# A graph network with a feed-forward part on chosen tokens: the choice made in two parts, the first during layer three

## The chip, the cores and the metric
The kernel runs on one core of a Trainium2 chip. The metric is the device time of one execution in microseconds (us). TensorE (PE) multiplies, VectorE (DVE), ScalarE (ACT) and GpSimd (POOL) do the rest of the arithmetic, SyncE (SP) issues most DMAs, GpSimd issues the indirect ones.

## What is computed
x has 6250 rows of 256. It is normalised, goes through three graph convolutions (200000 edges and a loop at each node), and is added to x. Then the rows are normalised again, half of them (less one) are chosen by a score, and these go through a feed-forward part and are added at their place:
```
x = x + gnn(layernorm(x))                    # relu after layers one and two
n = layernorm(x)
weights = n @ wr + br                        # one score a row
sel_idx = top_k(weights, 3125)[:3124]
h = gelu(n[sel_idx] @ w1 + b1)               # 256 -> 1024
y = (h @ w2 + b2) * weights[sel_idx]         # 1024 -> 256
out = x + n + zeros.at[sel_idx].set(y)
```

## The kernel before
The nodes are 49 tiles of 128 rows. A layer's sum over the edges is a product with the adjacency matrix: for the 32 or 34 fullest rows of tiles ("dense", 49 matmuls of 128x128 by 128x512 in f16 each) it is held as f16 tiles, for the others ("sparse") rows are gathered from DRAM by GpSimd (`fetch_row`, L1434) and summed with one-hot matrices (L958; the one-hots by VectorE at L753). One such matmul is a **unit**; a table puts 5798 units of the three layers in one order, dense and sparse ones mixed, and layer three begins at unit 3830. All that stands beside them is placed by unit numbers: the sum of a finished tile (`sum_tile`, L736 and L738) and the addition of x (`add_x`, L777 and L781) at `SUM_AT`, the loads for it (`fetch_extra`) at the sum of two tiles before. `norm_group` (L783 to L809, with a root on ScalarE, L1218) normalises a group of tiles right behind the sum of its last tile; the groups have `NORMS` = 7, 7, 7, 7, 7, 7, 5, 2 tiles in the order in which they end, and the sums that close them stand at units 4184, 4465, 4723, 5026, 5267, 5565, 5743 and 5798. 75 units later SyncE stores them (`store_pairs`, L1571 and L1572: normalised row and base row, side by side, into `pair_dram`). `sum_tile` frees the PSUM bank of its tile. All sparse tiles use one bank, so the start of a sparse tile waits for the sum of the sparse tile before it: the starts at units 5054, 5273, 5383, 5488, 5593 and 5699 wait for the sums at 5041, 5252, 5361, 5467, 5580 and 5677.

When the layer ends, the block of `graph` ends (every engine waits for all), and `finish` begins. SyncE loads w1 and w2 and stores out's base rows, 6.1 MB in one DMA (L1666, and L1668 for the rest). VectorE finds the score from which 3124 rows are chosen: it counts the scores above a bound (L1691), then in eight rounds above 15 (at last 7) trial bounds at once (L1696 to L1699); TensorE adds up the partitions (L1799), VectorE reads the counts (L1701 to L1703). Two matmuls (L1801, L1802) count ties and places, VectorE spreads each chosen row over slot numbers (L1709 to L1726, one-hot tiles at L1726), 49 matmuls (L1807) turn that into the list, and GpSimd gathers the listed rows of `pair_dram` (L1785), 25 slots of 128 rows (the last 52). The slots are taken in blocks of 1 and then 4 (`BLOCKS`). Per block: TensorE turns the rows (`turn`, L1816), VectorE copies them out of PSUM (`settle`, L1736), TensorE makes eight hidden sums (`hidden`, L1827, four PSUM banks), ScalarE gelu (L1864). Then the output sums of the block before (`outputs`, L1838, eight matmuls a slot), VectorE's gate (`weigh`, L1742 and L1744) and addition (`put`, L1749 and L1751), and GpSimd's store into out (L1791).

Of the kernel before, what the change touches and what calls it, by code (L numbers as in the profile page):

```python
# [8 lines left out]
ALU = mybir.AluOpType  # L9
ACT = mybir.ActivationFunctionType  # L10
AX = mybir.AxisListType
# [5 lines left out]
P = 128  # L17
# [116 lines left out]
NORMS = (7, 7, 7, 7, 7, 7, 5, 2)  # L134
# [4 lines left out]
BLOCKS = [range(0, 1)] + [range(c, min(c + BLOCK, SLOTS)) for c in range(1, SLOTS, BLOCK)]  # L139
BLOCK_OF = {s: (c, s - b[0]) for c, b in enumerate(BLOCKS) for s in b}  # L140
# [45 lines left out]
SUM_AT = sum_units()  # L186
TURN_AT = [u + 12 for u in SUM_AT]
# [82 lines left out]
PAIR_OUT_AT = [SUM_AT[2 * TILES + NORM_FROM[g + 1] - 1] + 75 for g in range(len(NORMS))]  # L270
# [17 lines left out]
BANK, BANK_BEFORE = bank_table()  # L288

# [17 lines left out]
def build(nc, x, x_turned, dst_rows, dst_over, dst_last, edges, gw, gb, wr, br, w1, b1, w2, b2, out):  # L307
    ctx = ExitStack()
    with ctx:
# [14 lines left out]
        with ExitStack() as inner:  # L324
            graph(nc, inner, space, gathered_in, ones, route, small, smalli, b1_sb, br_b, x, x_turned, dst_rows, dst_over, dst_last, edges, gw, gb, wr, br, b1, b2,
                  pair_dram)
        finish(nc, space, gathered_in, ones, route, small, smalli, pair_dram, br_b, w1, b1_sb, w2, out)


def graph(nc, ctx, space, gathered_in, ones, route, small, smalli, b1_sb, br_b, x, x_turned, dst_rows, dst_over, dst_last, edges, gw, gb, wr, br, b1, b2, pair_dram):  # L330
# [58 lines left out]
    def items_of(l):  # L389
# [17 lines left out]
    SLOT_OF = (3,) + tuple((TD - 4 + m) % ASLOTS for m in range(1, 4))  # L407
# [51 lines left out]

    (c_init, c_pool, c_dve, last_in, over_in, first_in, weights_in, later_in) = (sem(n) for n in (  # L460
# [25 lines left out]
    (m_v, m_p, stat_s, root_s, norm_s, pairs_out, x_added) = (sem(n) for n in (  # L486
        "m_max", "m_all", "stat_step", "root", "xn_ready", "pairs_stored", "x_added"))
# [19 lines left out]
    first_bank = [both[:, 0:D], ag[2][:, 0:D]]  # L507
    steps = {"all": 0}

    def bank(q):  # L510
        return (ag[0][:], ag[1][:], ag[2][:], pw[0][:, 0, :], pw[0][:, 1, :], pw[1][:, 0, :])[BANK[q]]

    with nc.Block() as block:
        @block.vector
        def _(dve):
# [12 lines left out]
            noted(dve.memset(ones16[:], 1.0), "ones")  # L528
            done(dve.memset(wrap[:], 0.0))
# [216 lines left out]
            def spot_steps(n):  # L746
                if n == 0:
                    dve.wait_ge(stored_0, 16)
                    dve.wait_ge(stored_s, 32)
                if n >= HOTS // 4:  # L750
                    dve.wait_ge(g_used, SPOT_GROUPS[n - HOTS // 4][1])
# [31 lines left out]
            def norm_group(g):  # L783
# [15 lines left out]
                if g:  # L799
# [1099 lines left out]
```

## Time and profile before
| | us |
|---|---|
| median of 3 runs | 2122.54 (2122.16 to 2124.14) |
| span of the profiled execution | 2111.3 |
| TensorE's matmuls busy | 1871.8 (89%) |
| VectorE busy | 1025.7 (49%) |
| ScalarE busy | 529.4 (25%) |
| GpSimd busy | 1152.2 (55%) |
| mean DMA rate | 190 GB/s |

The span is that of one execution, and the median is of other, unprofiled ones; 11.2 us lie between them. A profile is read from the page (shares of the whole span) to the views of single stretches: the chain of work that ended last names what released what; the windows give each engine's busy time in a stretch, with the clock that TensorE was granted (1.00 is 2.4 GHz, 0.50 is 1.2 GHz); the waits list what TensorE stood still for; the timeline lists instructions with their start, length, and in brackets the idle time before them and what ended it.

### The profile page before, as it was taken

The page shows a single profiled execution, that of the slowest core. Times are in us where ns is not written, and L with a number is a line of the kernel's source. Part 1 is how long each engine was busy: PE and PEld are TensorE (multiplying, and loading weights), DVE is VectorE, ACT ScalarE, POOL GpSimd, SP SyncE. Part 2 cuts the span into 40 slices and gives each one's busy share as a digit, 9 for nine tenths or more (in the row PEclk, how much of TensorE's full clock was granted, in tenths as well). Part 3 has the DMA queues.
Part 4 walks back from the last instruction along what each step waited for, and adds up shares of the span by engine and source line. Part 5 has one row for each costly group of instructions (what it writes and reads, how often), then busy time and mean ns, then how long its engine had stood idle before and what let it go on. Part 6 is the DMA issues. An engine that isn't in the chain of part 4 may idle for free. (4 is left out here: it accounts for less than half of the span.)

```text
span 2111.3 us, 28622 instructions
## 1 busy us (share of the span) xinstructions
PE 1871.8 (89%) x10097; PEld 1069.4 (51%) x10097; DVE 1025.7 (49%) x3169; ACT 529.4 (25%) x1126; POOL 1152.2 (55%) x1218
## 2 busy tenths in 40 slices
PE   6874879989999999897999999998999899828998
PEld 5752556655555566444554544443444344314666
DVE  7777888867666666322222222202555443572212
ACT  5814234433444455301111111100000000002110
POOL 5400656766676666134777777724777677404111
PEclk9965899999999999999999999999999999968999
DMA  7647045445555665745677677655888688454000
GB/s 253 201 149 267 16 152 172 155 156 165 166 198 195 197 204 179 268 161 177 227 237 243 223 231 244 228 170 195 290 287 291 209 293 289 151 196 124 21 15 24
DMA packets 166993, 402.10 MB, mean 190 GB/s; under 512 B 28651, under 2 KB 118945, under 8 KB 154056
## 3 DMA queue, kind: packets, MB, share of 16 engines
q1 hardware_dynamic: 116264, 262.16, 35.2%
q0 software_dynamic: 50592, 138.13, 21.3%
q8 instruction: 84, 1.38, 0.3%
q14 instruction: 53, 0.43, 0.1%
HBM read 284.18 MB, written 116.01 MB: 190 GB/s over the span
## 5 line engine op out<-in xcount | busy, mean ns | idle before, releaser
L1434 POOL DMA_INDIRECT space_rows<-row_dram,src_s x947 | 962.7, 1017 | 394.5 <-issue 209.9
L946 PE MATMUL ag<-space_a,space_ring 128*128 128x512 f16 x2107 | 628.7, 382 | 22.1 <-POOL space_ring L1442 22.1
L914 PE MATMUL pw<-space_tables 128*128 128x147 f16 (+1 forms) x2022 | 330.1, 248 | 53.7 <-DVE space_tables L714 45.2
L958 PE MATMUL ag<-space_rows,hots 128*128 128x512 f16 x947 | 359.7, 380 | 3.0 <-DVE hots L753 1.5
L914 PEld LDWEIGHTS pw<-space_tables 128*128 128x128 f16 x2022 | 219.1, 116 | 240.3 <-DVE space_tables L714 70.6
L714 DVE TENSOR_TENSOR space_tables<-iota_two,space_tables 128x294 f16<-128x294 f16 (+1 forms) x1011 | 304.7, 335 | 0.0
L1190 ACT ACTIVATE space_ring<-pw 128x784 f16<-128x784 f32 (+1 forms) x257 | 220.4, 858 | 309.4 <-PE pw L914 305.5
L946 PEld LDWEIGHTS ag<-space_a,space_ring 128*128 128x128 f16 x2107 | 198.8, 97 | 125.3 <-issue 19.4
L711 DVE TENSOR_TENSOR space_tables<-iota_many,space_tables 128x512 f16<-128x512 f16 x506 | 215.1, 425 | 52.0 <-PE pw L914 49.5
L946 PE MATMUL pw<-space_b,space_ring 128*128 128x512 f16 x784 | 205.2, 382 | 8.1 <-DVE space_work L738 8.1
L946 PE MATMUL pw<-space_a,space_ring 128*128 128x512 f16 x686 | 173.3, 385 | 0.0
L1200 ACT ACTIVATE space_work<-space_work,per_node 128x256 f32<-128x256 f32 x147 | 73.3, 503 | 315.0 <-DMA space_work<-extra 315.0
L958 PEld LDWEIGHTS ag<-space_rows,hots 128*128 128x128 f16 x947 | 107.3, 113 | 86.5 <-DMA space_rows<-row_dram,src_s 5.7
L743 DVE SCALAR_TENSOR_TENSOR space_a<-both,per_node,space_a 128x256 f16<-128x256 f32 x49 | 23.7, 484 | 230.4 <-ACT space_a L1214 230.4
L1208 ACT ACTIVATE space_work<-both,gb_sb 128x128 f32<-128x128 f32 x196 | 61.4, 364 | 250.8 <-PE both L964 250.7
L946 PEld LDWEIGHTS pw<-space_b,space_ring 128*128 128x128 f16 x784 | 77.2, 99 | 92.5 <-DVE space_work L738 8.6
L946 PEld LDWEIGHTS pw<-space_a,space_ring 128*128 128x128 f16 x686 | 67.9, 99 | 82.0 <-issue 5.3
L753 DVE TENSOR_TENSOR hots<-iota_many,key_s 128x512 f16<-128x512 f16 x238 | 105.9, 461 | 1.5
L946 PE MATMUL ag<-space_b,space_ring 128*128 128x512 f16 x392 | 105.0, 384 | 0.0
L1442 POOL TENSOR_TENSOR space_ring<-space_ring,ident 128x128 f16<-128x128 f16 x34 | 22.1, 652 | 150.6 <-ACT space_ring L1194 93.6
L972 PE MATMUL both<-gw_sb,space_work 128*128 128x256 f32 x392 | 101.4, 381 | 0.0
L1791 POOL DMA_INDIRECT out<-space_a,space_rows x24 | 23.4, 973 | 141.3 <-DVE space_a L1751 141.3
(351 smaller groups left out, 1895.4 us busy)
## 6 DMA issues: line engine op xcount, KB each, us to landing
space_ring<-adj SPq DMA_DIRECT2D x49, 1568.0 KB, 7.6
adj<-space_ring SPq DMA_DIRECT2D x34, 1568.0 KB, 6.1
space_tables<-adj SPq DMA_DIRECT2D x17, 1568.0 KB, 7.6
extra<-hots SPq DMA_DIRECT2D x3, 6272.0 KB, 23.1
space_work<-extra SPq DMA_DIRECT2D x147, 128.0 KB
space_rows<-row_dram,src_s POOLq DMA_INDIRECT x947, 3.8
space_b<-in_x_turned SPq DMA_DIRECT2D x7, 896.0 KB, 13.8
space_a<-in_x SPq DMA_DIRECT2D x7, 896.0 KB, 6.1
```

The costliest lines, as they stand in the source:

```text
L711: dve.tensor_tensor(olo[:, r // 2], iota_many[:], slo[:, 2 * j:2 * j + 4].unsqueeze(1).broadcast_to([P, P, 4]), ALU.is_equal)
L714: dve.tensor_tensor(ohi[:, r, 0:n], iota_two[:, 0:n], key[:, 2 * j:2 * j + 2].unsqueeze(1).broadcast_to([P, n, 2]), ALU.is_equal).then_inc ...
L743: dve.scalar_tensor_tensor(hh[l][:, t, D:2 * D], ph[:, 0:D], factor[:, l, t:t + 1], hh[l][:, t, 0:D], ALU.mult, ALU.subtract).then_inc(lo_ ...
L753: dve.tensor_tensor(hots_area[:, n % (HOTS // 4)], iota_many[:], key_s[:, s:s + 4].unsqueeze(1).broadcast_to([P, P, 4]), ALU.is_equal).the ...
L914: pe.matmul(pw[v % 2][:, half, at_c:at_c + n], olo[:, j % RING // 2, :, j % 2 * 2 + i], ohi[:, j % RING, 0:n, i], start=s == FIRST[w], sto ...
L946: mm = pe.matmul(bank(q), a[:, k, :], hh[l][:, k, :], start=i == 0 and not own, stop=i == TILES - 1)
L958: pe.matmul(bank(q), hots_area[:, hot_at, :, g - SPOT_GROUPS[SPOT_GROUP_OF[g]][0]], slots[g % GR], start=False, stop=i == n).then_inc(g_us ...
L972: mm = pe.matmul(ph[:, 0:D], fresh[:, q % 2, f, :], gw_sb[:, l, f, :], start=f == 0, stop=f == HALVES - 1)
L1190: act.activation(target[:, :, d:d + n].rearrange("p s (h d) -> p s h d", h=2), pw[v % 2][:, :, 0:n // 2 * TILES].rearrange("p h (d s) -> p ...
L1200: act.activation(ep[:, q % 2], ep[:, q % 2], ACT.Copy, scale=unfactor[:, l, t:t + 1]).then_inc(e_scaled, 1)
L1208: ins = act.activation(fresh[:, q % 2, f, :], px[:, f * P:(f + 1) * P], ACT.Relu, bias=gb_sb[:, l, f:f + 1])
L1434: pool.indirect_dma_start(slots[g % GR], None, row_dram[STEP_LAYER[g]], bass.IndirectOffsetOnAxis(src_s[:, s:s + 1], 0)).then_inc(g_in[g % ...
```

## The change
The first 38 tiles to be normalised (six groups) hold 38 tiles' scores; the 11 others have 1460 rows (tiles 27 to 33 and 45 to 48). Of the 38 tiles' rows the best 3124 - 1460 = 1664 (13 slots) belong to the chosen ones whatever the others' scores are. They are chosen during layer three (`begin_choice`, `after_count`, `spread` and `take_list` on VectorE, `count_choice`, `ties` and `listing` on TensorE, all with 0 for the first choice), at fixed units: counts at 5440, 5462 and so on to 5616, ties at 5638, the list at 5693, four turns at 5770 to 5788, their copies at 5792. The remaining 1460 rows (12 slots) are chosen from all the rest in the same manner, with the steps put between hidden sums and output sums of the first slots. The blocks are now 4, 3, 3, 3 slots and, of the second choice, 4, 4, 4. Turns of later slots stand behind single hidden sums or output sums (`TURN_IN_HIDDEN`, `TURN_IN_OUT`), hidden sums use three banks. `NORMS` is 7, 7, 7, 7, 5, 5, 7, 4, and the groups stand at 4184, 4465, 4723, 5026, 5204, 5382, 5696 and 5798; each is stored 70 units later, with a third DMA for each tile that stores out's base rows. There is one block for all: no barrier behind layer three. w1 and w2 are loaded at units 5686 and 5745. The late tiles' part of `pair_dram` is filled with zeros early on, so that every row holds a number.

The tables and the code of the engines, cut to its core:
```diff
-NORMS = (7, 7, 7, 7, 7, 7, 5, 2)
+NORMS = (7, 7, 7, 7, 5, 5, 7, 4)
+EARLY_GROUPS = 6
+EARLY = sum(NORMS[:EARLY_GROUPS])
...
+FIRST_SLOTS = (KEEP - UNSEEN) // P
+CHOSEN = (FIRST_SLOTS * P, KEEP - FIRST_SLOTS * P)
...
+COUNT_SPACE = 22
+COUNT_AT = [SUM_AT[2 * TILES + EARLY - 1] + 58 + COUNT_SPACE * r for r in range(COUNTS_OF_CHOICE)]
+TIES_AT = COUNT_AT[-1] + COUNT_SPACE
+LISTING_AT = TIES_AT + 55
+ROWS_TURN_AT = [UNITS - 28 + 6 * s for s in range(len(BLOCKS[0]))]
+ROWS_SETTLE_AT = UNITS - 6
...
-PAIR_OUT_AT = [SUM_AT[2 * TILES + NORM_FROM[g + 1] - 1] + 75 for g in range(len(NORMS))]
+PAIR_OUT_AT = [u + 70 for u in NORM_AT]
...
+            def after_count(ph, r):
...
+                dve.wait_ge(s_count, COUNTS_OF_CHOICE * ph + r + 1)
...
+                    dve.tensor_reduce(part[:, 0:n], flags[:, 0:n], AX.X, ALU.add).then_inc(s_part, 1)
...
+            def settle(s):
+                (c, i), n = BLOCK_OF[s], width(s)
+                if s == FIRST_SLOTS:
+                    dve.wait_ge(pairs_late, 48 * (TILES - EARLY))
+                dve.wait_ge(x_t, s + 1)
...
             upto(UNITS + 300)
+            begin_choice(1)
+            for c in range(len(BLOCKS) + 1):
+                if c < len(BLOCKS) and c != SECOND:
+                    hidden_turns(c)
+                for s in BLOCKS[c - 1] if c else ():
+                    weigh(s)
+                for s in BLOCKS[c - 1] if c else ():
+                    put(s)
+                    for k in CHOICE_IN_OUT.get(s, ()):
+                        choice_part(k)
+                    for e in TURN_IN_OUT.get(s, ()):
+                        settle(e)
+                if c == SECOND:
+                    hidden_turns(c)
...
+            def count_choice(ph, r):
+                n = ROUNDS[r - 1][1] if r else 1
+                pe.wait_ge(s_part, COUNTS_OF_CHOICE * ph + r + 1)
+                pe.matmul(choice_count[:, 0:n], ones[:], choices[ph]["part"][:, 0:n], start=True, stop=True,
+                          skip_group_check=True).then_inc(s_count, 1)
...
+            def hidden(c):
+                n = width_of(c)
+                pe.wait_ge(x_s, ended(c))
+                for m in range(HM):
+                    h = c * HM + m
+                    if h >= 3:
+                        pe.wait_ge(h_act, h - 2)
...
+                    mm.then_inc(h_mm, 1)
+                    for k in CHOICE_IN_HIDDEN.get((c, m), ()):
+                        choice_part(k)
+                    for s in TURN_IN_HIDDEN.get((c, m), ()):
+                        turn(s)
...
+            pool.wait_ge(pairs_out, 48 * EARLY)
+            pool.wait_ge(c_dve, steps["list 0"])
+            for s in BLOCKS[0]:
+                fetch_chosen(s)
+            pool.wait_ge(agg_d, len(DENSE_Q))
+            for s in range(len(BLOCKS[0]), FIRST_SLOTS):
+                fetch_chosen(s)
+            pool.wait_ge(pairs_late, 48 * (TILES - EARLY))
+            for s in range(STORED_BEFORE):
+                store_chosen(s)
+            pool.wait_ge(c_dve, steps["list 1"])
+            for s in range(FIRST_SLOTS, SLOTS):
+                fetch_chosen(s)
+            for s in range(STORED_BEFORE, SLOTS):
+                store_chosen(s)
...
-                    sp.dma_start(pair_dram[t * P:t * P + P, 0:D], xn[:, i]).then_inc(pairs_out, 16)
-                    sp.dma_start(pair_dram[t * P:t * P + P, D:2 * D], nodes[:, t]).then_inc(pairs_out, 16)
+                    sp.dma_start(pair_dram[t * P:t * P + P, 0:D], xn[:, i]).then_inc(stored, 16)
+                    sp.dma_start(pair_dram[t * P:t * P + P, D:2 * D], nodes[:, t]).then_inc(stored, 16)
+                    sp.dma_start(out[t * P:t * P + m, :], nodes[0:m, t]).then_inc(stored, 16)
```

Three places in the engines' order of instructions. First, VectorE in layer three near unit 5565. Before, behind the sum that closes the group of seven tiles (L787 to L809 is the group, L736 and on the next sum):
```order
L787 BN_STATS stats<-space_b 128x6 x7
L792 BN_AGGR aggr<-stats 128x2 x7
L795 TENSOR_SCALAR rstd_x<-aggr 128x7
L798 RECIPROCAL rstd_x<-rstd_x 128x7
L802 TENSOR_SCALAR space_tables<-space_b,aggr,rstd_x 128x256 x7
L807 TENSOR_TENSOR space_b<-space_b,space_tables 128x256 x7
L809 SCALAR_TENSOR_TENSOR moments,route<-space_tables 128x256 x7
L753 TENSOR_TENSOR hots<-iota_many,key_s 128x512
L736 SCALAR_TENSOR_TENSOR space_b<-ag,per_node,space_work 128x256
L738 SCALAR_TENSOR_TENSOR space_b<-ag,per_node,space_b 128x256
L777 TENSOR_TENSOR space_b<-space_b,space_work 128x256
```
In the changed kernel, in the same stretch of units (L893 to L939 is a sum, L911 one-hots, L999 to L1008 a round of the choice):
```order
L939 TENSOR_TENSOR space_b<-space_b,space_tables 128x256
L911 TENSOR_TENSOR hots<-iota_many,key_s 128x512
L999 TENSOR_SCALAR space_b<-both 128x15
L1001 TENSOR_SCALAR space_b<-space_b 128x1
L1002 TENSOR_TENSOR space_b<-space_b 128x1
L1005 TENSOR_TENSOR space_b<-trial_masks,space_b 128x15
L1006 TENSOR_TENSOR space_b<-space_b 128x735
L1008 TENSOR_REDUCE space_b<-space_b 128x15
L893 SCALAR_TENSOR_TENSOR space_b<-ag,per_node,space_work 128x256
L895 SCALAR_TENSOR_TENSOR space_b<-ag,per_node,space_b 128x256
L935 TENSOR_TENSOR space_b<-space_b,space_work 128x256
```
The group of 7 tiles has moved away from between two sums, and one round of the choice stands between them.

Second, TensorE in the feed-forward part, before (L1827 hidden sums, L1838 output sums, L1816 turns):
```order
L1827 MATMUL fp<-space_b,space_tables 128x512 x16
L1838 MATMUL fp<-space_tables,space_ring 128x256 x32
L1816 MATMUL fp<-space_rows,space_a 128x128 x8
L1827 MATMUL fp<-space_b,space_tables 128x512 x16
L1838 MATMUL fp<-space_tables,space_ring 128x256 x32
L1816 MATMUL fp<-space_rows,space_a 128x128 x8
L1827 MATMUL fp<-space_b,space_tables 128x512 x16
```
In the changed kernel, about the last counts of the second choice (L1340 hidden sums, L1353 output sums, L1327 turns, L1293 counts, L1299 and L1300 ties):
```order
L1340 MATMUL ag<-space_b,space_ring 128x384 x2
L1293 MATMUL both<-space_rows,ones 128x15
L1340 MATMUL pw<-space_b,space_ring 128x384 x4
L1353 MATMUL ag<-space_tables,space_a 128x256 x8
L1293 MATMUL both<-space_rows,ones 128x7
L1327 MATMUL pw<-ident,space_a 128x128 x2
L1353 MATMUL pw<-space_tables,space_a 128x256 x8
L1299 MATMUL both<-space_rows,tri 128x98
L1300 MATMUL both<-space_rows,ones 128x98
L1327 MATMUL ag<-ident,space_a 128x128 x2
L1353 MATMUL ag<-space_tables,space_a 128x256 x8
```
Turns stood in a row between blocks and now stand one by one behind sums, with the steps of the choice among them.

Third, VectorE in the feed-forward part. Before, the end of a block (L1749 and L1751 put a slot, L1736 settles turned rows):
```order
L1749 TENSOR_TENSOR space_work<-fp,space_tables 128x256
L1751 SCALAR_TENSOR_TENSOR space_a<-space_work,space_rows,space_a 128x256
L1749 TENSOR_TENSOR space_work<-fp,space_tables 128x256
L1751 SCALAR_TENSOR_TENSOR space_a<-space_work,space_rows,space_a 128x256
L1749 TENSOR_TENSOR space_work<-fp,space_tables 128x256
L1751 SCALAR_TENSOR_TENSOR space_a<-space_work,space_rows,space_a 128x256
L1736 COPY space_b<-fp 128x2x128 x3
L1736 COPY space_b<-fp 128x2x52
```
In the changed kernel, the end of the second choice's spread (L1032 to L1040; L1056 settles, L1069 and L1071 put):
```order
L1032 TENSOR_TENSOR space_rows<-iota,space_rows 128x588
L1034 TENSOR_TENSOR space_rows<-space_rows,tile 128x49x12
L1035 TENSOR_SCALAR space_rows<-space_rows,part_f 128x49x12
L1040 TENSOR_TENSOR space_ring<-iota_many,space_rows 128x512 x12
L1040 TENSOR_TENSOR space_ring<-iota_many,space_rows 128x128
L1056 COPY space_b<-ag 128x2x128
L1069 TENSOR_TENSOR space_work<-ag,space_tables 128x256
L1071 SCALAR_TENSOR_TENSOR space_a<-space_work,gate,space_a 128x256
L1056 COPY space_b<-pw 128x2x128
```
The settling of turned rows, which stood at once behind the puts, now also stands behind the spread of the second choice.

## Rows read from the trace of the kernel before
**Rows 1.** the page: span of the profiled execution and instructions
```profile
span 2111.3 us, 28622 instructions
```

**Rows 2.** timeline, end of layer three (start us, us, engine line op out<-in xcount)
```profile
1843.95 1.73 DVE L787 BATCH_NORM_STATS2 stats<-space_b 128x6 f32<-128x256 f32 x5
1852.70 0.48 DVE L736 SCALAR_TENSOR_TENSOR space_b<-ag,per_node,space_work 128x256 f32<-128x256 f32 x1
1847.19 6.64 PE L946 MATMUL pw<-space_a,space_ring 128*128 128x512 f16 x30
```

**Rows 3.** the chain that ended last: start us, us, what
```profile
1911.01 6.50 PE fp L1827 x32
1955.54 13.83 PE fp L1838 x64
1969.39 0.44 DVE space_work L1749
1970.82 0.42 PE fp L1816 x2
1972.08 14.00 PE fp L1827 x32
2063.53 11.97 PE fp L1827 x32
2075.50 27.77 PE fp L1838 x128
```

**Rows 4.** windows: stretch and us, busy of five engines, PEclk, DMA share, GB/s
```profile
1770.00:1792.00 22.00, 22.00 (x103) 10.21 (x102) 5.69 (x12) 1.02 (x2) 16.52 (x19) 1.00 0.76 263
1808.00:1812.00 4.00, 3.97 (x12) 1.54 (x13) 1.88 (x4) 0.51 (x1) 0.94 (x1) 0.64 0.20 66
1863.00:1909.00 46.00, 10.72 (x71) 8.20 (x71) 31.95 (x96) 1.28 (x1) 7.10 (x21) 0.50 0.56 191
1939.00:1943.00 4.00, 3.48 (x7) 1.50 (x8) 3.25 (x14) 0.00 (x0) 1.01 (x1) 0.69 0.09 34
1969.00:1972.00 3.00, 1.53 (x10) 0.88 (x8) 2.31 (x7) 0.00 (x0) 0.98 (x1) 1.00 0.01 4
```

**Rows 5.** waits of TensorE: us in total, times, longest us
```profile
PE ag L952 <- DVE space_b L738: 19.9, 3, 9.6
```

**Rows 6.** timeline around the stall near unit 5565, VectorE and TensorE
```profile
1792.46 0.48 DVE L736 SCALAR_TENSOR_TENSOR space_b<-pw,per_node,space_work 128x256 f32<-128x256 f32 x1 [10.61 <-PE pw L946]
1794.41 2.38 DVE L787 BATCH_NORM_STATS2 stats<-space_b 128x6 f32<-128x256 f32 x7
1808.03 0.61 PE L952 MATMUL ag<-space_a,ident 128*128 128x512 f16 x1 [9.57 <-DVE space_b L738]
```

**Rows 7.** timeline of one round of the choice
```profile
1869.26 0.17 DVE L1701 TENSOR_SCALAR_CACHE_REDUCE space_rows<-fp 128x15 f32<-128x15 f32 x1 [0.70 <-PE fp L1799]
1871.03 0.92 DVE L1699 TENSOR_REDUCE space_rows<-space_ring 128x15 f32<-128x735 f32 x1
1872.00 0.61 PE L1799 MATMUL fp<-space_rows,ones 128*128 128x15 f32 x2 [2.78 <-DVE space_rows L1699]
```

**Rows 8.** timeline of the list behind the last count
```profile
1894.38 0.26 DVE L1709 COPY space_rows<-fp 128x98 f32<-128x98 f32 x1 [1.26 <-PE fp L1802]
1897.29 1.44 DVE L1720 TENSOR_TENSOR space_ring<-space_rows 128x1225 f16<-128x1225 f16 x1
1900.88 4.31 DVE L1726 TENSOR_TENSOR space_ring<-space_rows 128x512 f16<-128x512 f16 x13
1901.35 4.11 PE L1807 MATMUL fp<-space_ring 128*128 128x50 f16 x49 [7.01 <-DVE space_ring L1726]
```

**Rows 9.** timeline of ScalarE at the start of the feed-forward part
```profile
1863.19 1.28 ACT L1856 ACT_TABLE_LOAD   x1 [5.10 <-PEq L513]
1921.62 0.69 ACT L1864 ACTIVATE space_ring<-fp,b_sb 128x512 f32<-128x512 f32 x1 [3.70 <-PE fp L1827]
```

**Rows 10.** timeline of SyncE, the stores of a seven-tile group begin
```profile
1690.51 0.84 SPq L1571 DMA_DIRECT2D pair_dram<-space_tables  x1
```

More of the change, by code:

```diff
@@ new lines, in choice_part, with hidden_turns @@
+            def choice_part(k):
+                if k < COUNTS_OF_CHOICE:
+                    after_count(1, k)
+                elif k == COUNTS_OF_CHOICE:
+                    spread(1)
+                else:
+                    take_list(1)
+            def hidden_turns(c):
+                for m in range(HM):
+                    for k in CHOICE_IN_HIDDEN.get((c, m), ()):
+                        choice_part(k)
+                    for s in TURN_IN_HIDDEN.get((c, m), ()):
+                        settle(s)
@@ new lines, in listing, with choice_part @@
+            def listing(ph):
+                for t in range(TILES):
+                    if t % 4 == 0:
+                        pe.wait_ge(s_hot, len(slots_hot) * ph + t // 4 + 1)
+                    mm = pe.matmul(listed[ph], slots_hot[t // 4][:, :, t % 4], choices[ph]["owned"][:, t].rearrange("p i c -> p (i c)"),
+                                   start=t == 0, stop=t == TILES - 1, skip_group_check=True)
+                mm.then_inc(s_list, 1)
+            def choice_part(k):
+                if k < COUNTS_OF_CHOICE:
+                    count_choice(1, k)
+                elif k == COUNTS_OF_CHOICE:
+                    ties(1)
+                else:
+                    listing(1)
@@ new lines, in output @@
+            def output(c, s):
+                i, n = BLOCK_OF[s][1], width(s)
+                if s >= 2:
+                    pe.wait_ge(y_t, s - 1)
+                for m in range(HM):
+                    mm = pe.matmul(bank_of(out_banks[s % 2])[0:n, 0:D], hid[c % 2][:, m, i * P:i * P + n], w2_sb[:, m, :],
+                                   start=m == 0, stop=m == HM - 1)
+                mm.then_inc(y_mm, 1)
+                for k in CHOICE_IN_OUT.get(s, ()):
+                    choice_part(k)
@@ L1131, in _ @@
             units(UNITS)
+            pe.wait_ge(w1_in, 16)
+            for c in range(len(BLOCKS) + 1):
+                if c < len(BLOCKS) and c != SECOND:
+                    hidden(c)
+                if c == 1:
+                    pe.wait_ge(w2_in, 16)
+                    pe.wait_ge(summed, 3 * TILES)
+                if c:
+                    pe.wait_ge(h_act, c * HM)
+                for s in BLOCKS[c - 1] if c else ():
+                    output(c - 1, s)
+                    for e in TURN_IN_OUT.get(s, ()):
+                        turn(e)
+                if c == SECOND:
+                    hidden(c)
         @block.scalar
```

583 lines of the change are left out of this document (313 added, 270 removed).

## The prediction, made before the changed kernel was run
> **What bounds the kernel now.** I read the page first [rows 1], then the chain of work that ended last [rows 3], the end of layer three [rows 2] and the busy shares by stretch [rows 4]. The reader is to see three stages. Up to 1853.83 us TensorE works through the table of units, back to back at the full granted clock (PE busy 22.00 of 22.00 us, in [rows 4]), so there an instruction added on TensorE costs its length and one added on an engine beside it costs nothing until TensorE waits for it. From 1853.83 to 1911.01 us, 57.2 us, TensorE has little to do: the last normalisation, the end of the block, nine counts, the list, the first gather. In most of that stretch VectorE works (31.95 of 46.00 us) and TensorE stands at a granted clock of 0.50. From 1911.01 to 2103.27 us, 192.3 us, TensorE bounds again, with the feed-forward part: the chain holds hidden sums, output sums and the short handovers between them. 8.0 us of tail follow to 2111.3. The median of the runs is 2122.54, so 11.2 us lie outside the profiled span; I make the sum on the span and add them at the end.
>
> There are also two long waits of TensorE in layer three, of 9.6 us at most each, for the sum at L738 [rows 5]. One begins behind the normalisation at unit 5026 and stays. The other is in [rows 6]: a normalisation of seven tiles starts at 1794.41 on VectorE, the sum of the sparse tile comes behind it (TensorE waited 9.57 us, to 1808.03), and the next sparse tile needs the same PSUM bank.
>
> **The change, part by part.**
>
> *Norm groups.* The group at unit 5565 is gone; its neighbours now stand at 5382 and 5696, and 5382 comes after the sum of 5361 that the sparse tile at 5383 needs. So the 9.57 us go. Behind them the clock was 0.64 for the 4 us of 1808 to 1812 [rows 4]: 4 x 0.36 = 1.4 us, with a little before that row 1.5. Gain 11.1. What is late next is the sum at 5580, 13 units (2.8 us) before its sparse start; a sum takes some 2 us on VectorE with its add, of which TensorE waits for the first 1.0: 0 to 1 us, I take 0.2.
>
> *First choice in layer three.* On TensorE nine counts, two matmuls for ties, 49 short ones for the list and four turns are inserted. A count reads 0.61 us from start to end in [rows 7], most of which is the fill of the array; between other matmuls I take 0.3: 2.7 us. Ties 0.7. The list took 4.11 at a granted clock of 0.50 [rows 4, 8]; with 26 instead of 50 columns and at 1.00 it lies between 2.0 (half) and 4.1, I take 2.8. A turn is 0.42 alone [rows 3], 0.35 among others: 1.4. Together 7.6. On VectorE a round costs 2.69 us (from 1869.26, where the count is read, to 1871.95, where the next partial counts are there, [rows 7]) and the counts stand 22 units = 4.74 us apart. The stretch of units in which they stand had VectorE busy 5.69 of 22.00 us [rows 4], 26%; with 2.69 in 4.74 it is 83%. It fits, but a sum that falls due behind a round is up to 2.7 us late. Sums with short distance are the ones of sparse tiles, of 21 units (4.5 us). I charge 2.0 us of waits in all: 0.5 for the first count, which stands behind a normalisation of five tiles (such a one took from 1843.95 to 1852.7, 8.7 us [rows 2], so 40 of the 58 units left for it), 0.5 for sums, 1.0 for the second turn, whose bank is read by VectorE only after the sum at 5768. The spread of the list (from 1894.38 to 1905.2, [rows 8]: 6.5 us of chain and 4.31 of hot tiles; of the chain the 3.6 us behind 1897.29 go by slots, so with 12 or 13 instead of 25 it is 4.7) fits into the 55 units = 11.9 us left for it. Layer three: -11.1 + 7.6 + 2.0 = -1.5; it ends at about 1852.3.
>
> *What leaves the path.* The 57.2 us between the stages: block end, counts, list and gather. The last two normalisation groups, their stores and the second choice move beside TensorE's hidden sums. Gelu's table load (1.28 us) and one activation (0.69, both [rows 9]) with the last root ahead of them stand before the fourth hidden sum, since there are now three banks and not four: 1.8 us. Nobody else waits: w1 and w2 are asked for at units 5686 and 5745, and four chosen rows are turned before the layer ends.
>
> *The feed-forward part on TensorE.* Hidden sums: 14.00 for a block of four slots (1972.08, [rows 3]), three of these; a block of three has 384 of 512 columns, 10.5, three of these; the last 11.97: 85.5. Output sums 13.83 per four slots and 27.77 for the last eight [rows 3]: 25 slots x 3.46 = 86.6. 21 turns x 0.35 = 7.4. The second choice's nine counts, ties and list: 2.7 + 0.7 + 2.8 = 6.2. Stalls: gelu's start 1.8. The spread is 12 hot instructions (4.31) and 4.7 us of chain, and VectorE must also put two slots (two operations of 0.44 each, [rows 3]) and settle two (a copy of that size); with the spread 11.8 us against 4.9 of TensorE's own work before it needs the settled rows for the hidden block behind: 6.9. Then the second part's first block and the last one 1.2 + 1.0, less than half of the 2.7 us from 1969.39 to 1972.08 that every block boundary takes now (put, turn, settle, [rows 3]; the changed order takes it away at the other boundaries, since turns stand inside running sums). 1.5 for one fall of the clock behind the long stall. Sum 198.1. So TensorE ends at 1852.3 + 198.1 = 2050.4, the span with the tail of 8.0 at 2058.4, the run at 2069.6. I predict **2070 us**, 52.9 less than now. Cross-check: the two last stages took 57.2 + 192.3 = 249.5 and take 198.1; with 1.5 from layer three that is 52.9.
>
> *Edits costed at nothing.* The stores of out's base rows: 49 more DMAs on SP, 6.4 MB. A group of seven tiles issues 14 DMAs, the first of 0.84 us [rows 10]; at that price 21 take 17.6 us, in which SP can't start `extra` loads. Those are asked for two tiles ahead, some 80 units or 17 us. If it were not hidden: DMA share is 0.76 at 263 GB/s in [rows 4]; 6.4 MB at 263 / 0.76 = 346 GB/s is 18.5 us, the upper bound. The lower is 0: the 6.1 MB that went out between the stages went beside the counts, and these are counted as gone already. I take 0, since share and rate have room. Pool's gathers of the chosen rows follow its last gather for layer three, with some 70 units (15 us) for four rows before their first turn. The second list must be read some 88 us into the last stage and its first rows are turned at 109: 21 us of cover for 3 us of landing.
>
> One rule of the Trainium skill speaks against this part. Here a trace of the spread (VectorE, 1897.29 to 1905.2) has no gather beside it [rows 8], so the rows don't show what it does to one. The Trainium skill, SBUF — State Buffer, in the warning on the "DVE blocks DMA" trap, states that while VectorE runs an operation in a two-port mode GpSimd can't write its descriptors. If that held here, Pool's stores and gathers beside the spread would be late by up to the 11.8 us of VectorE's work; the cover of 21 us takes that, so the sum is the same by the rule.
>
> **The rivals.**
>
> A, VectorE bounds the mixed stage. Per output slot of TensorE (3.46 + turn 0.35 + count 0.3 = 4.1 us) VectorE has a put 0.9, a settle 0.4, a weighing 0.65 (operations of the size of 0.44 and a small one) and a round 2.69: 4.6 us. For: it is in order and a count waits behind puts. Against: only four of nine counts and the list's parts stand in such places, the others stand in hidden sums where VectorE is nearly idle. If each of the first choice's and second choice's 18 counts is late by 1.1 us: +20, **2090 us**.
>
> B, the clock. Three gaps of like length are seen: behind 9.6 us at 1808 the clock was 0.64, behind the handover at 1937 to 1940 it was 0.69 over the next 4 us, behind the same handover at 1969 to 1972 it stayed at 1.00 [rows 4]. So one short gap in some of them costs 1.5 us. There are 22 places at which TensorE now waits on VectorE for a choice step; if each costs that: +33, **2103 us**. The trace gives it to few, since later boundaries held 1.00. The Trainium skill (TensorE: Matmul & The Clock Gate, "A second HAM failure mode: psum-queue depth-cycling") tells of a kernel whose clock went up and down from small idle times between groups of matmuls; that is this rival, and by that rule the time would be 2103; the trace agrees in one of the two short gaps.
>
> C, the second choice isn't hidden. Its list comes too late for slot 13 and TensorE stands: eight rounds of 3.39 (2.69 and the 0.70 that VectorE waits, [rows 7]) and 9.0 of spread, 36 us, **2106 us**. It would need a stop in front, as of the first gathers or stores on Pool.
>
> D, slower than before. Every sparse tile's start waits for the sum of the sparse tile before, in one bank. VectorE's rounds, roots and spreads are inserted between sum and start at five places (5273, 5383, 5488, 5593, 5699). If each of them stalls as that of [rows 6] does, 9.57 and 1.5 for the clock: 5 x 11.1 = 55.5, **2125 us**. It decides from five stalls on, since 52.9 / 11.1 = 4.8. Against: of the groups only one seven-tile one is within 20 units of such a start, and it comes after its sum.
>
> **How the numbers follow.** My forecast has 0.58, A 0.20, B 0.10, C 0.07, D 0.04; 0.01 is left for a time within 0.2% (4 us), about what a measurement can tell from no change. The forecast's own bounds: terms that could be less (waits of layer three 2 to 0, stall at the spread 6.9 to 2, list 2.8 to 2.0 twice) sum to -8.5; upward, counts at 0.61 (+5.6), lists at 4.1 (+2.6), stores half of 18.5: some +17, of which I take 12, since not all fall together. With A inside, and a part of B, the range is 2060 to 2092. Faster 0.95, same 0.02, slower 0.03.
>
> **What would show it.** Right: no wait over 3 us of TensorE near unit 5593; layer three's last matmul ends near 1852; the first hidden sum starts less than 2 us behind it; granted clock 1.00 there; one stall of 5 to 8 us for VectorE's settle behind the spread; 13.83 or 14 us per block as now. A: waits of TensorE on the partial counts (the reduce) of more than 1 us at most places. B: clock under 0.9 in many 4-us pieces. C: a wait on the gather of slot 13. D: L738 among the waits more than four times with 9 us. The prediction is wrong if the last stage takes more than 215 us, or layer three ends behind 1865.

## The result, and the profile after
| | before | changed |
|---|---|---|
| median, us | 2123.34 (4 runs, 2122.16 to 2125.57) | 2066.92 (4 runs, 2062.73 to 2070.45) |
| span of the profiled execution | 2111.3 | 2061.0 |
| last unit of layer three ends | 1853.8 | 1858.8 |
| first hidden sum starts | 1911.0 | 1858.6 |
| TensorE's last matmul ends | 2103.3 | 2051.7 |

The ratio is 0.974, 95% interval 0.9723 to 0.9757: 56.4 us less, where 52.9 were forecast (2070 us, range 2060 to 2092). One number above needs a correction: the 11 late tiles have 1386 rows (ten of 128 and the last of 106). So the best 3124 - 1386 = 1738 early rows are certain; the kernel takes 13 full slots of them, 1664, and 1460 is the number of rows that the second choice takes.

What TensorE waits for from 1640 us to the end, as the waits of the changed kernel list it (us in total, times, longest; one more entry has 0.2 us):
```profile
PE ag L1252 <- DVE space_b L895: 9.5, 1, 9.5
PE ag L1340 <- DVE space_b L1056: 8.3, 2, 7.3
PE pw L1327 <- DVE space_b L1056: 1.7, 2, 1.0
PE ag L1340 <- ACT space_ring L1709: 1.2, 1, 1.2
PE pw L1340 <- DVE space_b L1056: 0.5, 1, 0.5
```
The first line answers to [rows 5]: L895 is the sum that was L738, and of its two long waits in layer three one is left, behind the group at unit 5026. No line names a partial count (`count_choice`, L1293): TensorE waits at none of the 18 counts. The rest is the settling of turned rows (L1056). The timeline of TensorE shows the start of the last stage and the longest wait in it (start us, us, and in brackets the idle time before):
```profile
1856.46 2.32 PE L1246 MATMUL pw<-space_a,space_ring 128*128 128x512 f16 x10
1858.62 1.88 PE L1340 MATMUL ag<-space_b,space_ring 128*128 128x512 f32 x4
...
1865.11 1.98 PE L1340 MATMUL ag<-space_b,space_ring 128*128 128x512 f32 x4 [1.18 <-ACT space_ring L1709]
...
1930.57 2.93 PE L1340 MATMUL ag<-space_b,space_ring 128*128 128x384 f32 x4 [7.30 <-DVE space_b L1056]
```
The hidden sum (L1340) follows the last unit (L1246) without a gap: the 57.2 us of [rows 2, 3] are gone. The start of gelu (the last root, the table load and the first activation on ScalarE) costs 1.18 us. Behind the spread stands the wait of 7.30 us. Windows of the changed kernel (columns as in [rows 4], the clock third from the end):
```profile
1845.00:1865.00 20.00, 18.03 (x74) 8.30 (x72) 12.10 (x39) 2.63 (x5) 4.73 (x5) 1.00 0.75 246
1930.60:1933.60 3.00, 3.00 (x5) 1.79 (x6) 0.00 (x0) 0.06 (x1) 0.83 (x1) 0.51 0.12 44
```
The clock holds 1.00 across the end of layer three, is 0.51 behind the wait of 7.30 us, and 1.00 again from 1960 to 1970, with waits of 1.0 and 0.5 us in it.

### The profile page after: what moved, and what is told of

Same layout as the page of the kernel before. It is cut to its first block, busy times and chain, and to the rows that moved or that the text cites. A ratio compares the mean times of both kernels' runs of the same rounds, so it can differ in the third digit from the quotient of the medians.

```text
span 2061.0 us, 28897 instructions
## 1 busy us (share of the span) xinstructions
PE 1861.0 (90%) x10168; PEld 1068.9 (52%) x10168; DVE 1054.3 (51%) x3267; ACT 528.7 (26%) x1126; POOL 1161.9 (56%) x1213
## 4 chain that ended last, share of the span: by engine, by line
PE 67%; POOL 10%; issue 9%; DVE 7%; DMA 5%; ACT 2%; POOLq 0%; DVEq 0%; ACTq 0%
PE ag L1246 21%; PE pw L1246 16%; PE ag L1258 9%; POOL space_rows L1835 6%; PE pw L1214 5%; PE both L1272 4%; PE pw L1340 3%; PE ag L1353 2%; PE pw L1353 2%; PE ag L1340 1%; PE both L1264 1%; POOL space_rows L1802 1%; POOL space_rows L1827 1%; DMA space_rows<-row_dram,src_s 1%; DMA extra<-space_tables 1%
## 5 line engine op out<-in xcount | busy, mean ns | idle before, releaser
L1246 PE MATMUL ag<-space_a,space_ring 128*128 128x512 f16 x2107 | 628.9, 382 | 30.5 <-POOL space_ring L1843 30.5
L1246 PEld LDWEIGHTS ag<-space_a,space_ring 128*128 128x128 f16 x2107 | 198.9, 98 | 133.5 <-issue 27.3
L868 DVE TENSOR_TENSOR space_tables<-iota_many,space_tables 128x512 f16<-128x512 f16 x506 | 215.2, 425 | 59.1 <-PE pw L1214 56.5
L1246 PE MATMUL pw<-space_b,space_ring 128*128 128x512 f16 x784 | 204.4, 381 | 6.4 <-DVE space_work L895 6.4
L1246 PE MATMUL pw<-space_a,space_ring 128*128 128x512 f16 x686 | 172.0, 381 | 1.9 <-DVE space_b L895 1.9
L1246 PEld LDWEIGHTS pw<-space_b,space_ring 128*128 128x128 f16 x784 | 77.0, 98 | 90.6 <-DVE space_work L895 6.9
L1246 PEld LDWEIGHTS pw<-space_a,space_ring 128*128 128x128 f16 x686 | 67.4, 99 | 80.1 <-DVE space_b L895 2.4
L911 DVE TENSOR_TENSOR hots<-iota_many,key_s 128x512 f16<-128x512 f16 x238 | 106.5, 463 | 1.4
L1246 PE MATMUL ag<-space_b,space_ring 128*128 128x512 f16 x392 | 105.2, 384 | 0.1
L893 DVE SCALAR_TENSOR_TENSOR space_work<-ag,per_node,space_work 128x256 f32<-128x256 f32 x78 | 37.7, 483 | 121.6 <-PE ag L1258 62.8
```

The costliest lines, as they stand in the source:

```text
L868: dve.tensor_tensor(olo[:, r // 2], iota_many[:], slo[:, 2 * j:2 * j + 4].unsqueeze(1).broadcast_to([P, P, 4]), ALU.is_equal)
L911: dve.tensor_tensor(hots_area[:, n % (HOTS // 4)], iota_many[:], key_s[:, s:s + 4].unsqueeze(1).broadcast_to([P, P, 4]), ALU.is_equal).the ...
L1246: mm = pe.matmul(bank(q), a[:, k, :], hh[l][:, k, :], start=i == 0 and not own, stop=i == TILES - 1)
```

## The experiments
Each kernel ran beside the kernel before on its chip. These runs used three chips (the number behind a label), and the kernel before took 2107.8 us (median) on the first, 2115.7 on the second, 2112.9 on the third. So kernels are compared by ratio, and by the lengths of four stages in their traces, of one execution each: A is from the start of tile sum 0 to that of sum 35 (in layer one), B from sum 35 to sum 135, C from sum 135 to the end of the last unit of layer three, D from there to TensorE's last end. All are in us. "Sum n" is the n-th, from 0, of the 147 tile sums in order of time, by the start of its first instruction (L736, in the changed kernel L893).

| kernel | median | ratio to before (95%) | A | B | C | D |
|---|---|---|---|---|---|---|
| before | 2123.3 | 1 | 454.1 | 1020.3 | 100.9 | 249.4 |
| changed | 2066.9 | 0.974 (0.9723, 0.9757) | 463.1 | 1020.1 | 95.6 | 192.9 |
| before_again (1) | 2101.0, 1 run | | 441.9 | 1018.7 | 102.4 | 248.6 |
| after_again (1) | 2052.7 | 0.9727 (0.9699, 0.9755) | 452.8 | 1017.7 | 95.6 | 195.4 |
| late_clear (1) | 2046.0 | 0.9696 (0.9672, 0.9721) | 445.7 | 1022.1 | 95.6 | 194.9 |
| no_base (1) | 2045.5 | 0.970 (0.9674, 0.9726) | 446.9 | 1019.7 | 95.4 | 194.4 |
| groups_only (2) | 2105.7 | 0.994 (0.9915, 0.9965) | 459.6 | 1017.9 | 90.8 | 250.6 |
| groups_even (2) | 2057.6 | 0.9728 (0.9713, 0.9744) | 458.6 | 1012.0 | 97.3 | 195.9 |
| spread_later (2) | 2053.7 | 0.9696 (0.968, 0.9712) | 462.9 | 1019.9 | 95.5 | 186.1 |
| all_three (2) | 2037.9 | 0.9634 (0.9606, 0.9662) | 462.8 | 1013.2 | 95.3 | 190.6 |
| after_third (3) | 2056.5 | 0.9715 (0.9674, 0.9756) | 459.5 | 1020.2 | 95.5 | 193.1 |
| late_clear_again (3) | 2052.8 | 0.9707 (0.9667, 0.9746) | 451.8 | 1017.7 | 95.6 | 195.1 |
| two_moved (3) | 2042.0 | 0.9657 (0.9614, 0.97) | 459.2 | 1007.3 | 97.3 | 188.3 |
| long_rounds (3) | 2074.3 | 0.9796 (0.9746, 0.9845) | 461.4 | 1018.2 | 107.5 | 204.5 |

**Both kernels again.** No edit. For the kernel before:

> The kernel before, unchanged, profiled a second time. The profiled execution of before had a span of 2111.3 us while its other runs took 2122 to 2126. Theory 'spread': the difference is between executions, not outside the span. Then this second profile has a span within 2 us of its own time (some 2113 to 2124), and the sum number 35 of the 147 tile sums (732.7 us in the first profile, 743.1 us in the changed kernel) starts anywhere from 732 to 743 us. Theory 'systematic': 11 us always lie outside the span, and that sum starts within 2 us of 732.7.

For the changed kernel, on the first and on the third chip:

> The changed kernel, unchanged, profiled a second time on the same chip as the three others. Layer three and the feed-forward part are set by an order of instructions: from sum 135 to the end of TensorE's work the time should be that of the first profile (288.5 us) within 1 us. If the 10.3 us that the changed kernel lost ahead of layer three are of this kernel, its sum 35 starts at 743 us again, within 2 us; if they come from the spread between executions, it can be 733. Time 2063 to 2070 us.

> The changed kernel once more, as the base for the three others on this chip. By the traces so far its time is set by how many gathers of the first layer take over 2 us (20 and 15 of them in two executions, sum 35 at 463.1 and 452.8 us behind sum 0); from sum 135 on 288 to 291 us.

The second profile of before has a span of 2099.3 us in a run of 2101.03, and the changed kernel's first 2061.0 in 2062.73: 1.7 us lie outside the span. That is theory "spread", by its first sign. Its second was missed: sum 35 started at 721.6 us, earlier than either theory said. The 11.2 us that the prediction added were 1.7 and, for the rest, a profiled execution that was shorter than the median.

The second profile of the changed kernel has sum 35 at 733.5 us and not at 743, so the 10.3 us are not lost in every execution. C and D took 291.0 us, 2.5 more than the first time where 1 was allowed; 1.5 of these are one wait, told under "Out's base rows not stored". The time of 2052.7 lies under the expected 2063 to 2070, on a chip on which the kernel before is faster too. On the third chip C and D took 288.6, where 288 to 291 were expected. C and D of one kernel agree between executions within 2.5 us; A moves, by 12 us between two executions of before and by 10 between three of the changed kernel.

One thing the medians and the traces don't agree on. C and D together are 59 to 62 us shorter than before, and the tail is 1.3 us longer; the medians gain 56.4, 55.1 and 56.4. So some 2 to 6 us (an estimate from these rows) are lost ahead of sum 135 or in the spread, and the traces can't tell which.

**Groups alone.** In the kernel before:
```diff
-NORMS = (7, 7, 7, 7, 7, 7, 5, 2)
+NORMS = (7, 7, 7, 7, 5, 5, 7, 4)
```


> The kernel before with one line of the change: the normalisation groups 7, 7, 7, 7, 5, 5, 7, 4. My account: the wait of 9.6 us for the sum behind unit 5565 goes, with some 1.5 us of slow clock; the last group has four tiles and not two, so the stretch from the end of layer three to the first hidden sum (57.2 us) is some 2.5 us longer. From sum 135 to the end of layer three: 100.9 - 11.1 = 89.8 us; time 8.6 us under the kernel before. Rival: the wait only moves to another sparse start, and from sum 135 to the end stays above 97 us, time as before.

C fell from 100.9 to 90.8 (89.8 expected), D rose by 1.1 (2.5 expected), the median by 10.0. The waits of TensorE, against [rows 5]:
```profile
PE ag L952 <- DVE space_b L738: 10.5, 2, 9.5
```
One wait of 9.6 us is gone and none came in its place. So some 10 us of the gain are the groups' and have nothing to do with the choice (the ratio is 0.994, 0.9915 to 0.9965).

**Groups at 4964 in place of 5026.** In the changed kernel:
```diff
-NORMS = (7, 7, 7, 7, 5, 5, 7, 4)
+NORMS = (7, 7, 7, 6, 6, 5, 7, 4)
```


> The changed kernel with groups 7, 7, 7, 6, 6, 5, 7, 4: the fourth closes at unit 4964 and not 5026, so no group stands between the sum at 5041 and the sparse start at 5054 that needs it. My account: the last wait for a sum of 9.5 us goes, with up to 1.9 us of slow clock behind it: layer three is 10 to 11.5 us shorter, all else alike, some 11 us (0.5%) less than the changed kernel. Rival: a new wait, at the start at 5273, whose sum at 5252 stands behind a group that now has six tiles: then 0 to 5 us are left of it.

The waits show that the 9.5 us are gone, and that no wait came at the start at 5273. But B fell by 6 to 8 us, not by 11, and 1.7 came back in C: the first count now waits 2.15 us for VectorE, and the clock is at 0.50 from 1763 to 1766, behind it. B and C together are 4 to 6 us shorter, 4 to 11 in the three traces with this edit; it is open where the rest of the 11 went. The ratio shows no gain (0.9728, where the changed kernel has 0.974, 0.9727 and 0.9715 on other chips).

**The spread one step later.** In the changed kernel, from the computed places:
```diff
+CHOICE_IN_OUT[5] = []
+CHOICE_IN_HIDDEN[3, 5] = []
+CHOICE_IN_HIDDEN[3, 0] = [9]
+CHOICE_IN_OUT[7] = [10]
```


> The changed kernel with ties and spread of the second choice one step on: behind the first hidden sum of the block of slots 10 to 12 (no settling is due in that block) and not behind the output sum of slot 5; the list behind the output sum of slot 7. My account: TensorE's 7.3 us at the first hidden sum of that block go and the fall of the clock behind it with 1.7 us, so the last stage takes 192.9 - 9 = 184 us. Rival 1: VectorE is late for the puts of slots 7 and 8 instead, and the wait moves to the third output sum behind it (3 to 7 us stay). Rival 2: the second list comes too late for slot 13, a wait on a gather of several us.

D is 186.1 and not 184. TensorE at the same hidden sum, where 7.30 us stood:
```profile
1922.87 1.56 PE L1344 MATMUL ag<-space_b,space_ring 128*128 128x384 f32 x4 [1.15 <-DVE space_b L1060]
```
1.15 us are left: even without the spread VectorE puts a slot (0.9 us, from 1921.54) before it settles the last turned row, at 1922.40; that is the term that the expectation had forgotten. Neither rival showed: no wait at slots 7 and 8 and none on a gather.

**Out's base rows not stored.**
```diff
-                    sp.dma_start(out[t * P:t * P + m, :], nodes[0:m, t]).then_inc(stored, 16)
```


> Leaves out the stores of out's base rows (49 DMAs, 6.4 MB), so out holds the chosen rows alone. It prices the edit that the prediction put at nothing. Theory: same as the changed kernel within 2 us. Rival: the stores load the DMA engines in layer three or SyncE's queue; then up to 18.5 us faster, by their transfer time.

The median is 7 us under after_again, but the trace says where: A is 5.9 shorter, in layer one, ahead of all these stores, while B, C and D differ by 2.0, -0.2 and -1.0. So the medians don't price the stores. The traces show a smaller cost that the prediction had not named. VectorE's last normalisation group writes the buffer from which the group before it is stored, and so waits until the last of those DMAs has landed, a base row's (timeline of VectorE, changed kernel):
```profile
1865.60 1.41 DVE L962 TENSOR_SCALAR space_tables<-space_b,aggr,rstd_x 128x256 f32<-128x256 f32 x4 [2.27 <-DMA out<-space_b]
```
The waits were 2.3, 4.4 and 2.5 us in three executions of the changed kernel, 5.7 in two_moved, 6.2 in all_three, and none in no_base. Settling stands behind this group, so TensorE's turn waits too: 0, 1.5 and 0 us in the three, 2.8 in two_moved, 3.4 in all_three, 0 in no_base. By this wait the stores cost 0 to 1.5 us in the changed kernel.

**The filling of the late rows moved.** The zeros are not written at the start; SyncE copies a finished tile into that part at the first pair stores of layer three:
```diff
-            for a, b in LATE_RUNS:
-                sp.dma_start(pair_dram[a * P:b * P, :].rearrange("(p t) (i d) -> p (t i) d", p=P, i=2),
-                             zeros.unsqueeze(1).broadcast_to([P, 2 * (b - a), D])).then_inc(pairs_clear, 16)
...
+                if g == 0:
+                    for a, b in LATE_RUNS:
+                        sp.dma_start(pair_dram[a * P:b * P, :].rearrange("(p t) (i d) -> p (t i) d", p=P, i=2),
+                                     nodes[:, t].unsqueeze(1).broadcast_to([P, 2 * (b - a), D])).then_inc(pairs_clear, 16)
```


> The zeros that fill the late tiles' part of pair_dram (2.9 MB, ahead of the first layer's row stores on SyncE, and waited for by VectorE's first one-hots) are replaced by a copy of a finished tile's rows, written at the first pair stores in layer three. Theory 'clear': the 10.3 us that the changed kernel is later at layer three come from these two DMAs and what queues behind them; then this kernel is some 10 us faster than the changed one, about 2057. Rival 'spread or other': the loss has another cause (the spread between executions, or GpSimd's order), and this kernel is within 3 us of the changed one, 2064 to 2070. In layer three the 2.9 MB cost nothing by either.

> The filling of the late tiles' part moved into layer three, again, with more rounds. Theory 'clear': 5 to 8 us under the changed kernel on this chip. Rival 'spread': within 3 us of it; then the 6.7 us between the medians of the first comparison were chance, and so is that the kernel that only left out the base rows was 7 us under it with the same code ahead of layer three.

The first time it was 6.7 us under the changed kernel, the second 3.7, between what the two theories said, and each time with intervals that overlap. A is 445.7, 451.8 and (in all_three) 462.8 with the filling moved, 446.9 to 463.1 in eight traces with it early, 441.9 to 459.6 in three traces of the early part of before. No stage of the traces decides it, and it stays open whether the early filling costs some us.

**All together.** The three edits in one, and two of them (without the moved filling):

> Groups 7, 7, 7, 6, 6, 5, 7, 4, the spread one step later, and the filling of the late tiles' part moved into layer three, all in one. If each is what I take it for they add: 11 + 9, and 0 to 8 for the early part, so 20 to 28 us under the changed kernel, a ratio to the kernel before of 0.961 to 0.964. If the early part's loss is only the spread between executions, 20.

> Groups 7, 7, 7, 6, 6, 5, 7, 4 and the spread one step later, the early part as in the changed kernel. My account: 8 us in layer three and 7 to 9 in the last stage less than the changed kernel: 15 to 17 us, 0.7 to 0.8%. Sum 35 to 135 some 1012 us, last stage some 186 to 190.

On the third chip two_moved took 2042.0 beside 2056.5 for the changed kernel: 14.5 us less, where 15 to 17 were expected. By the traces it is 12.9 us less in B (8 expected), 1.8 more in C, where the first count waits 1.86 us, and 4.8 less in D (7 to 9 expected): the turn behind the last normalisation waits 2.8 us, which takes back part of what the later spread gives. all_three has the lowest ratio of all, 0.9634 (0.9606, 0.9662), as expected (0.961 to 0.964), and within the interval of two_moved. Both are faster than the kernel before, and than the changed kernel by some 0.7 to 1%: two_moved beside it on one chip, all_three by ratios whose intervals don't meet.

**Longer rounds.**
```diff
-                    done(dve.tensor_tensor(flags[:, 0:n], score.unsqueeze(1).broadcast_to([P, n, TILES]),
+                    for _ in range(3):
+                        done(dve.tensor_tensor(flags[:, 0:n], score.unsqueeze(1).broadcast_to([P, n, TILES]),
```


> Each of the 16 rounds of the choice makes its comparison three times: 1.9 us more of VectorE in each of 16 rounds (less in the last of each choice), 29 us in all. It asks how much cover VectorE has left (rival A). If TensorE never waits for partial counts, as in the changed kernel, and the cover is large, the time stays within 3 us. By my account a round in layer three is then 4.6 us of 4.74, so rounds and sums come into each other's way there: waits of 1 to 3 us at several counts and at the start at 5488 or 5593, and 0 to 1 us at counts beside hidden sums: 8 to 15 us slower than the changed kernel. If VectorE bounded this stage already, all of it would show: 29 us.

Missed: C grew by 12.0 us and D by 11.4, 23 of the 29 us added (by the medians on this chip 17.8). The timeline of TensorE in it:
```profile
1797.88 0.40 PE L1294 MATMUL both<-space_b,ones 128*128 128x15 f32 x2 [2.25 <-DVE space_b L1009]
...
1815.95 0.39 PE L1253 MATMUL ag<-space_a,ident 128*128 128x512 f16 x1 [2.96 <-DVE space_b L895]
...
1904.94 0.40 PE L1294 MATMUL both<-space_rows,ones 128*128 128x15 f32 x2 [2.94 <-DVE space_rows L1009]
```
and its windows:
```profile
1816.00:1820.00 4.00, 4.00 (x13) 1.61 (x14) 3.69 (x12) 0.51 (x1) 1.04 (x1) 0.60 0.24 69
1905.00:1909.00 4.00, 4.00 (x13) 3.25 (x14) 3.76 (x11) 0.00 (x0) 0.99 (x1) 0.57 0.09 33
```
Rival A is a real bound that lies close: with 1.9 us more a round VectorE holds TensorE at counts and at a sparse start (L1253), and behind the waits of 2.96 and 2.94 us the clock falls besides, which the expectation had left out. By these windows that loses 1.6 and 1.7 us; the wait of 2.25 us was followed by a clock of 1.00.

## Why the prediction was right
**What bounds.** As read: three stages, of which the second is gone. D fell from 249.4 to 192.9, that is 56.5, beside 51.4 forecast. No run divides this among its parts (the block end, the choice moved beside other work, the weights loaded early). The trace of before gives a guide to it: of its 57.2 us, 9.4 pass from the last unit to the first instruction of `finish` on VectorE (1863.2), some 42 to the end of the list at 1905.5, and 5.5 to the first hidden sum.

**Layer three.** The wait behind 5565: -11.1 forecast, -10.1 in groups_only (-11.6 against the second trace of before). What the first choice puts in: 7.6 + 2.0 = 9.6 forecast, 95.6 - 90.8 = 4.8 measured, by C of the changed kernel against groups_only. All its terms were too large. Of the nine counts eight delay the matmuls behind them by 0.13 us and the first by 0.24, 1.2 us together, where 2.7 were taken. The two matmuls for ties are 0.4 (0.7 taken), the four turns 0.9 (1.4 taken). With 26 columns and the full clock the list is, on TensorE:
```profile
1832.22 1.75 PE L1307 MATMUL both<-space_b,space_ring 128*128 128x26 f16 x49
```
1.75 us, of which 1.6 delay what follows, while I took 2.8 out of bounds of 2.0 to 4.1: under the lower one. The bounds came from a misread row. The 4.11 us of [rows 8] are not the matmuls' own time: they go beside VectorE's 13 instructions for the one-hot tiles (4.31 us), and in the trace the matmuls start in fours, 0.33 us apart, each four 0.05 us behind a tile. Within a four they are 0.041 us apart, and in the changed kernel, where all tiles are ready, all 49 are 0.033 us apart. The waits were 0.2 and 0.7 us, not 2.0.

**The last stage.** 198.1 forecast, 192.9 measured (195.4, 193.1 in two more). The wait behind the spread: 6.9 forecast, 7.30. The second part's start: 1.2, measured 1.02 and 0.52. Before the last block 1.0, measured 0.96. Gelu's start: 1.8, measured 1.18, more of it lay beside the first three hidden sums. Too large were the turns and counts. Output sums with a turn and a count between them, in the chain of the changed kernel (start us, us):
```profile
1885.38 3.45 PE ag L1353 x16
1889.23 3.46 PE pw L1353 x16
```
They start 3.84 us apart, of which the sum is 3.45: a turn and a count are 0.39 together, and I had taken 0.35 + 0.3. For 21 turns and 9 counts that is some 4 us. The list is again 1 us less, and hidden sums of full blocks take 13.8, without the start-up in the 14.00 of [rows 3].

**Edits costed at nothing.** The stores cost 0 to 1.5 us, by a wait that I had not named: the buffer of the normalised rows, freed by the landing of the base rows' DMAs. The prediction looked at SyncE's queue and the DMA engines' share, and not at who waits for the semaphore that the new DMAs also feed. The early part was left out of the sum; the pair of profiles shows 10.2 us of loss ahead of sum 135, of which the runs can't say how much is the change's.

**The sum.** In the spans it is 2061.0 against 2058.4: +10.2 ahead of sum 135, -3.8 from there to the end of layer three, -5.2 in the last stage, +1.3 in the tail (9.3 us, not 8.0). Then 11.2 were added, of which 1.7 are outside the span. That 2070 lies so near 2066.9 is in part luck: these errors offset each other. The gain, which doesn't hang on that constant, was 52.9 forecast and 56.4 measured, and here too errors meet: C and D together gave 61.8 us, 8.9 more than forecast, of which the early part and the tail took back what the prediction had put at nothing.

**Rivals.** A did not happen (no wait at any count) but long_rounds shows it less than 1.9 us a round away. B: one fall of the clock behind the 7.30 us, none elsewhere in the last stage. Its price of 1.5 us a fall is near what is seen (3 us at 0.51 behind the 7.30 us, 1.6 and 1.7 us in long_rounds), but TensorE waited at few of the 22 places. The prediction called its three gaps of like length; they are 9.57, 1.10 and 1.03 us. C: no wait on a gather. D: five starts and no stall at any of them (the one sum that still holds TensorE is that of before).

## What to carry to other kernels
A serial choice (count, compare, count) hardly costs when its steps stand between matmuls of another stage, at a distance of more than one round; its price is then the few short matmuls and whatever one long stretch on VectorE delays. Place that long stretch where nobody needs that engine's short work; here the move of it by one step made the last stage 7 to 9 us shorter. When a transfer is added to a group that already has a semaphore, look at who waits for that semaphore, not only at the queue.

## What was not expected of the hardware
**Long gathers.** The spread between executions sits in layer one, and with it goes the number of gathers issued by GpSimd that take over 2 us instead of 0.95: 7 of them (22 us in all) in the execution of before with A = 441.9, 10 (26 us) with 446.9, 17 (55 us) with 454.1, 20 (61 us) with 463.1. It is no strict order: 13 (43 us) stand beside 459.6 and 12 (39 us) beside 462.9, and 13 (39 us) beside 451.8. So it is not shown that the long gathers make the difference. Such gathers are rare elsewhere, but one stands in layer three of the changed kernel, beside the first choice's one-hot tiles, and at the same place in 8 of the 11 traces of this kernel and its variants, each time of 4.93 or 4.94 us. The timeline of before in layer one:
```profile
446.44 5.87 POOL L1434 DMA_INDIRECT space_rows<-row_dram,src_s  x1 [0.30 <-PE ag L958]
```
and of the changed kernel in layer three, VectorE and GpSimd:
```profile
1825.80 4.30 DVE L1040 TENSOR_TENSOR space_ring<-iota_many,space_b 128x512 f16<-128x512 f16 x13
```
```profile
1825.67 0.95 POOL L1835 DMA_INDIRECT space_rows<-row_dram,src_s  x1 [0.30 <-issue]
1826.92 4.94 POOL L1835 DMA_INDIRECT space_rows<-row_dram,src_s  x1 [0.30 <-issue]
```
The gather of 4.94 us stands beside back-to-back f16 operations with two inputs, as VectorE runs them in layer one all the time (5.61 of 5.70 us beside the gather of 5.87). It ends 0.8 us behind the last of these f16 operations (two of L911 follow the one-hot tiles, to 1831.04). The Trainium skill (SBUF — State Buffer, the warning on the "DVE blocks DMA" trap) says that GpSimd can't write descriptors while VectorE runs an operation in a 2-port mode, and names an f32 copy as one that does. The operations here are two-input f16 ones, and no run shows in which mode they ran. A gather held until VectorE is through would look like the one of 4.94, but not each is held: the one of 0.95 in the rows above began 0.13 us ahead of the one-hot tiles and ended beside them; in the three other traces all three gathers that began beside these tiles took 1.03 to 1.11 us (after_again, from 1814.93 on); and from 454 to 460 us in before the gathers took 0.95 to 1.11 us with VectorE busy 5.96 of 6.00 us, mostly with such operations. No run tried the cause. TensorE waited for no gather in that stretch, since the gathers are issued well ahead.

**The clock.** How long a wait was doesn't tell alone whether the clock fell behind it. In layer three and behind it, waits of 2.94 us and more were followed by 0.60, 0.57 and 0.51 (long_rounds, the changed kernel), and by 0.50 from 1869 to 1872 in all_three (3.42 us). Shorter ones went either way, as two waits of TensorE in two_moved show, with the windows behind them:
```profile
1758.24 0.38 PE L1297 MATMUL both<-space_b,ones 128*128 128x1 f32 x2 [1.86 <-DVE space_b L992]
1859.62 0.41 PE L1331 MATMUL pw<-ident,space_a 128*128 128x128 f32 x2 [2.78 <-DVE space_b L1060]
1759.00:1762.00 3.00, 3.00 (x8) 1.06 (x7) 2.86 (x7) 0.00 (x0) 2.39 (x3) 0.50 0.60 150
1860.00:1864.00 4.00, 4.00 (x13) 2.12 (x12) 0.42 (x1) 1.27 (x2) 0.00 (x0) 1.00 0.47 128
```
Behind the wait of 1.86 us the clock was 0.50, behind that of 2.78 it was 1.00; behind one of 1.88 us in all_three (1765.76) it was 1.00 too. In the kernel before, one of the five alike handovers (1.0 to 1.1 us) was followed by a fall: the one at 1937 in the first trace ([rows 4]), the one at 2017 in the second. So a wait can cost more than its own length, and a short one may cost it in one execution or place and not in another.
